# Attention inner loop: turns of four key tiles in place of pairs of two

## The reference

```python
DIM_HEAD, HEADS = 64, 16
q = (x @ Wq).reshape(b, s, HEADS, DIM_HEAD).transpose(0, 2, 1, 3)
k = (x @ Wk).reshape(b, s, HEADS, DIM_HEAD).transpose(0, 2, 1, 3)
v = (x @ Wv).reshape(b, s, HEADS, DIM_HEAD).transpose(0, 2, 1, 3)
scale = 1.0 / np.sqrt(np.sqrt(DIM_HEAD))
scores = jnp.einsum('bhqd,bhkd->bhqk', q * scale, k * scale)
weights = jax.nn.softmax(scores.astype(jnp.float32), axis=-1)
out = jnp.einsum('bhqk,bhkd->bhqd', weights, v)
return out.transpose(0, 2, 1, 3).reshape(b, s, HEADS * DIM_HEAD) @ Wo
```

## Time and profile before

| what | value |
|---|---|
| median of 3 runs | 3771.01 us (3770.84 to 3777.43) |
| time of the profiled execution | 3775.72 us |
| its span, first to last instruction | 3773.7 us |
| mean granted TensorE clock over the span | 0.954 |
| the two attention loops (first to last exponential) | 812.9 to about 2087 us, about 2187 to 3465.9 us |
| PE busy, 1200 to 1400 us | 199.43 of 200 us |
| DVE, ACT, POOL busy, 1200 to 1400 us | 124.77, 99.36, 174.44 us |
| copies of a finished group's output, first batch, 853.0 to 1464.6 us | 16, so 40.77 us a group |

### The profile page before, as it was taken

One profiled execution on the slowest core, in us unless ns is written; L12 is line 12 of the kernel. 1 busy time (PEld: TensorE's weight loads), 2 busy tenths in 40 slices (PEclk: granted clock), 3 DMA queues, 4 the chain that ended last, 5 costly groups with the idle time before them and its releaser, 6 DMA issues. The chain is left out here.

```text
span 3773.7 us, 48349 instructions
## 1 busy us (share of the span) xinstructions
PE 3348.8 (89%) x19009; PEld 1769.9 (47%) x19009; DVE 2411.6 (64%) x2756; ACT 1687.3 (45%) x2053; POOL 2768.3 (73%) x1154
## 2 busy tenths in 40 slices
PE   5674577379999999999999599999999999998798
PEld 2222222235554545455455245454554545454798
DVE  5998599766666665665664466666665665662554
ACT  4331433134454545445445345454545445544454
POOL 1783078238888888888889378888888888898233
PEclk9997799779999999999999799999999999999899
DMA  1330133010000000000000100000000000000000
GB/s 25 134 117 17 59 116 117 11 45 1 4 1 4 1 4 4 1 4 1 1 1 1 39 3 1 4 4 1 4 1 4 1 4 2 1 1 12 26 18 15
DMA packets 61536, 76.14 MB, mean 20 GB/s; under 512 B 7290, under 2 KB 48963, under 8 KB 61251
## 3 DMA queue, kind: packets, MB, share of 16 engines
q1 hardware_dynamic: 59362, 72.71, 6.0%
q10 hardware_dynamic: 1952, 0.43, 0.1%
HBM read 66.30 MB, written 6.82 MB: 19 GB/s over the span
## 5 line engine op out<-in xcount | busy, mean ns | idle before, releaser
L1311 POOL TENSOR_TENSOR den_g<-den_g,p 128x1024 f32<-128x1024 f32 x896 | 2129.0, 2376 | 292.4 <-ACT p L1287 184.8
L971 DVE TENSOR_REDUCE quarters<-psum 128x2 f32<-128x1024 f32 x1024 | 1250.3, 1224 | 941.8 <-PE psum L964 932.3
L1287 ACT ACTIVATE p<-psum 128x1024 f32<-128x1024 f32 x1024 | 994.8, 1023 | 725.8 <-PE psum L1190 719.5
L1201 PE MATMUL psum<-p,v 128*64 128x512 f32 x4096 | 991.4, 605 | 0.0
L964 PE MATMUL psum<-k_main,q_main 64*128 64x512 f32 x2048 | 462.5, 447 | 13.4 <-DVE quarters L971 10.9
L1201 PEld LDWEIGHTS psum<-p,v 128*64 128x64 f32 x4096 | 248.4, 136 | 469.7 <-issue 316.4
L1190 PE MATMUL psum<-q_main,k_main 64*128 64x512 f32 x2048 | 407.8, 394 | 4.5 <-PEq L1101 4.5
L1190 PE MATMUL psum<-q_rest,k_main 64*128 64x512 f32 x2048 | 404.7, 391 | 0.0
L1190 PE MATMUL psum<-q_main,k_rest 64*128 64x512 f32 x2048 | 404.5, 390 | 0.0
L1190 PE MATMUL psum<-row_shift,row_ones 64*128 64x512 f32 x2048 | 404.0, 389 | 0.0
L964 PEld LDWEIGHTS psum<-k_main,q_main 64*128 64x128 f32 x2048 | 193.6, 184 | 362.7 <-issue 198.6
(11 more groups left out here) (252 smaller groups left out, 3406.7 us busy)
## 6 DMA issues: line engine op xcount, KB each, us to landing
c_sb<-bc_rows SPq DMA_DIRECT2D x64, 512.0 KB, 3.5
work<-bc_rows SPq DMA_DIRECT2D x32, 512.0 KB, 4.9
resid<-in_resid SPq DMA_DIRECT2D x8, 256.0 KB, 3.3
x_mid<-resid SPq DMA_DIRECT2D x8, 256.0 KB, 2.6
xa<-x_mid SPq DMA_DIRECT2D x8, 256.0 KB, 3.5
x_tok<-x_mid SPq DMA_DIRECT2D x8, 256.0 KB, 3.7
x_mid<-x_tok SPq DMA_DIRECT2D x8, 256.0 KB, 2.7
x<-x_mid SPq DMA_DIRECT2D x8, 256.0 KB, 2.7
```

What stands on the lines that cost most here:

```text
L971: return nc.vector.reduce_max(quarters[:, :, n], max_banks.rearrange("p (h k) -> p h k", h=2), X_AXIS)
L1201: last = nc.tensor.matmul(o_bank[hi(h), :], vv[:, kt, hi(h)], p[:, u % LIVE, h, :], start=(kt == 0), stop=(kt == KT - 1))
L1287: nc.scalar.activation(flat(p[:, u % LIVE]), s_bank(u), ACT.Exp, scale=float(DH) ** -0.5).then_inc(p_ready, 1)
L1311: nc.gpsimd.tensor_tensor(sums, first, src, ALU.add).then_inc(added_g, 1)
```

## The change

TensorE's order is rewritten in turns of four units. In a turn, the 16 score steps of units first+2 to first+5 come in a row, with the four maxima of units first to first+3 before score steps 0, 5, 11 and behind step 15 (`MAX_AT`), then the values of the four units. A use of bank 7 stands either before the values of a turn or behind them. The jobs are renamed: each group has projections 0 and 1 (keys and queries, one each in turns 0 and 3, before the values) and "values" (turn 1, behind); `den` is behind turn 0, `out` before the values of turn 2, `shift` behind turn 2. Scores wait for the exponential at their first step and for the shift at their fourth. `LIVE` goes from 8 to 10. ScalarE and VectorE do their parts in the matching order: VectorE reads the four maxima of a turn, then does its parts of the bank's jobs and `make_shift`. The numbers of matmuls, exponentials, adds, readings and DMAs are the same.

```diff
-LIVE = 8
+LIVE = 10
...
-BANK7_AT = {0: 0, 2: "den", 8: "out", 10: "shift", 12: 1, 14: 2}
+TURN = 4
+TURNS = KT // TURN
+LEAD_S = 2
+
+BANK7_AT = {(0, "before"): 0, (0, "behind"): "den", (1, "behind"): "values", (2, "before"): "out",
+            (2, "behind"): "shift", (3, "before"): 1}
+
+MAX_AT = (0, 5, 11, 16)
...
-                def scores(u):
+                def score_steps(u):
...
-                    if kt == 0 and g:
-                        pe.wait_ge(shift_read, 2 * g)
-                    if u >= 2:
-                        pe.wait_ge(p_ready, u - 1)
...
                     for i, (left, right) in enumerate(terms):
+                        if i == 0 and u >= 2:
+                            pe.wait_ge(p_ready, u - 1)
+                        if i == 3 and kt == 0 and g:
+                            pe.wait_ge(shift_read, 2 * g)
                         for h in range(2):
                             last = nc.tensor.matmul(s_bank(u)[:, piece(h)], left[hi(h)], right[hi(h)],
                                                     start=(i == 0), stop=(i == len(terms) - 1))
-                    last.then_inc(s_psum, 1)
+                        if i == len(terms) - 1:
+                            last.then_inc(s_psum, 1)
+                        yield
...
-                scores(0)
-                scores(1)
-                for u in range(0, len(units), 2):
-                    maxes(u)
-                    if u + 2 < len(units):
-                        scores(u + 2)
-                        scores(u + 3)
-                    maxes(u + 1)
-                    values(u)
-                    values(u + 1)
-                    if u in at_unit:
-                        use_bank7(at_unit[u])
+                for u in range(LEAD_S):
+                    for _ in score_steps(u):
+                        pass
+                for i in turns:
+                    first = i * TURN
+                    ahead = range(first + LEAD_S, min(first + LEAD_S + TURN, len(units)))
+                    steps = (step for u in ahead for step in score_steps(u))
+                    for n in range(MAX_AT[-1] + 1):
+                        if n in MAX_AT:
+                            maxes(first + MAX_AT.index(n))
+                        next(steps, None)
+                    if (i, "before") in at_turn:
+                        use_bank7(at_turn[i, "before"])
+                    for u in range(first, first + TURN):
+                        values(u)
+                    if (i, "behind") in at_turn:
+                        use_bank7(at_turn[i, "behind"])
...
+                for i in turns:
+                    if (i - 1, "behind") in at_turn:
+                        read_bank7(at_turn[i - 1, "behind"])
+                    if i and i % TURNS == 0:
+                        copy_outputs(i // TURNS - 1)
+                    for u in range(i * TURN + LEAD_S, min((i + 1) * TURN + LEAD_S, len(units))):
+                        weigh(u)
+                    if (i, "before") in at_turn:
+                        read_bank7(at_turn[i, "before"])
...
+                for i in turns:
+                    g = i // TURNS
+                    for u in range(i * TURN, (i + 1) * TURN):
+                        if u in max_units:
+                            to, n = max_step(*units[u])
+                            dve.wait_ge(max_psum, u + 1)
+                            read_max(nc, quarters[:, to % 2], max_banks, n).then_inc(max_read, 1)
+                    k = at_turn.get((i, "before"))
+                    if k is not None and uses[k][0] == "out":
+                        add_outputs(k)
+                    elif k is not None:
+                        take_rest(k)
+                    if i % TURNS == SHIFT_MADE_AT // TURN and g + 1 < GC:
+                        dve.wait_ge(max_read, g * KT + SHIFT_MADE_AT)
                         if g:
                             dve.wait_ge(bank7_full, use_of["shift", g - 1] + 1)
                         make_shift(nc, st, quarters[:, (g + 1) % 2], maxima[:], shift).then_inc(shift_ready, 1)
...
+                    if (i - 1, "behind") in at_turn and uses[at_turn[i - 1, "behind"]][0] == "den":
+                        invert(g - 1)
+                        normalise(g - 1)
```

More of the change, by code:

```diff
@@ L1112, in attention_pairs @@
     units = [(g, kt) for g in range(GC) for kt in range(KT)]
+    turns = range(GC * TURNS)
     uses = []
[L1115 to L1126, removed]
+    for i in turns:
+        g = i // TURNS
+        for place in ("before", "behind"):
+            what = BANK7_AT.get((i % TURNS, place))
+            if what in ("den", "out"):
+                if g:
+                    uses.append((what, g - 1, i, place))
+            elif what == "shift":
+                if g + 1 < GC:
+                    uses.append((what, g, i, place))
+            elif what is not None and g + CHUNKS < GC:
+                uses.append((what, g, i, place))
+    at_turn = {(i, place): k for k, (what, g, i, place) in enumerate(uses)}
+    use_of = {(what, g): k for k, (what, g, i, place) in enumerate(uses)}
+    projection = lambda what, g: 2 * CHUNKS + g % CHUNKS if what == "values" else 2 * (g % CHUNKS) + what
     max_units = [u for u, (g, kt) in enumerate(units) if max_step(g, kt)[0] < GC]
@@ L1155, in _ @@
                     if pair:
-                        sp.wait_ge(bank7_full, use_of[2, CHUNKS * pair - 1] + 1)
+                        sp.wait_ge(bank7_full, use_of[1, CHUNKS * pair - 1] + 1)
                     for i, w in enumerate(("Wq", "Wk", "Wv")):
@@ L1205, in use_bank7 @@
                 def use_bank7(k):
-                    what, g, _ = uses[k]
+                    what, g, _, _ = uses[k]
                     if k:
@@ L1224, in use_bank7 @@
                             pe.wait_ge(weights, 48 * (g // CHUNKS))
-                        last = project(nc, bank7, w, xaT, 3 * (g % CHUNKS) + what)
+                        last = project(nc, bank7, w, xaT, projection(what, g))
                     last.then_inc(bank7_full, 1)
-                scores(0)
-                scores(1)
-                for u in range(0, len(units), 2):
-                    maxes(u)
-                    if u + 2 < len(units):
-                        scores(u + 2)
-                        scores(u + 3)
-                    maxes(u + 1)
-                    values(u)
-                    values(u + 1)
-                    if u in at_unit:
-                        use_bank7(at_unit[u])
+                for u in range(LEAD_S):
[15 more added lines that the diff above has]
+                        use_bank7(at_turn[i, "behind"])
             @block.scalar
@@ L1264, in read_bank7 @@
                     else:
-                        i = 3 * (g % CHUNKS) + what
+                        i = projection(what, g)
                         if i < 2 * CHUNKS:
@@ L1279, in copy_outputs, with weigh @@
                     nc.scalar.copy(o_raw[:], o_bank).then_inc(o_copied, 1)
-                for u, (g, kt) in enumerate(units):
+                def weigh(u):
                     act.wait_ge(s_psum, u + 1)
@@ L1350, in add_outputs @@
                         nc.vector.tensor_tensor(attnT[:, cols], attnT[:, cols], bank7, ALU.add).then_inc(bank7_free, 1)
-                for u, (g, kt) in enumerate(units):
-                    if kt == SHIFT_MADE_AT and g + 1 < GC:
-                        dve.wait_ge(max_read, u)
+                for i in turns:
+                    g = i // TURNS
+                    for u in range(i * TURN, (i + 1) * TURN):
[10 more added lines that the diff above has]
+                        dve.wait_ge(max_read, g * KT + SHIFT_MADE_AT)
                         if g:
```

## The result

The changed kernel takes 3926.86 us (median of 4 runs, 3924.5 to 3934.31) against 3772.59 for the kernel before, a ratio of 1.041 with a 95 % interval of 1.0392 to 1.0429: 4.1 % slower, 154 us. The forecast was 199 us and 3970 us, in a range of 3855 to 4035. The profiled executions differ by 158.6 us (3934.31 and 3775.72). All of it lies in the two attention loops, which take 163 us more; the rest of the program takes 5 us less. From its first to its last exponential a batch takes 1360.9 us (819.7 to 2180.6) and 1361.3 (2268.5 to 3629.8), against 1279.8 (812.9 to 2092.7) and 1279.0 (2186.9 to 3465.9) before.

What follows compares the result with a forecast made beforehand. TensorE was taken as the bound, busy 199.4 of 200 us in the attention loops. Terms: 203 (turns) + 4 (exponentials) - 20 + 12 (bank 7) = +199 us, forecast 3970 us, range 3855 to 4035.

Steps and rivals of the forecast that it cites:

- The mechanism: In a turn, each next maximum waits until VectorE has read the one bank pair: +203 us, longer turns' gain included.
- The handover's size: From one maximum's start to the next: 0.54 to the reading, 1.23 reading, 0.10 release, 1.87 us; low 1.71, high 1.92.
- halves: A maximum's two matmuls, taken to start one after the other behind values or a wait, 0.50 us for the pair.
- Bank 7: In the new places 56 projections and 40 sums of denominators no longer wait, 0.12 and 0.32 us each: -20 us.
- two new ones: Near waits at "values" behind turn 1 and the shift behind turn 2, 0.1 us each in 62 groups: +12 us.
- late shift: Rival: adding the outputs or `make_shift` ends 0.5 us later, each group waits: +31 us, 4001 us; chance 0.08.
- whole add: `make_shift`'s last instruction could wait for a whole GpSimd add, shift late by up to about 0.3 us a group, 19 us.
- The exponentials: At score step 8, hidden behind waiting maxima; in 11 turns without maxima 0.4 us short twice a turn: about +4 us.
- the trip: A turn of four saves one of two trips from scores to values and back: -0.37 us a turn.
- The exponential rival: The exponential, not the reading, holds TensorE up: turn 8.73 against 8.72 us, only bank 7's 20 us left, 3751; chance 0.05.
- The clock: Rival: TensorE's short pauses make the granted clock fall; low for a twentieth of the time, +100 us, 4071 us; chance 0.04.

Runs made afterwards that it cites:

- e8: The changed kernel with the maxima before score steps 0, 8 and 12 and behind step 15: 3990.69 us, ratio 1.0569 to the kernel before.
- e4: The changed kernel with maxima before steps 0 and 8, behind 15, and the fourth between the second and third unit's values: 3820.78 us, ratio 1.0125.
- e1: The changed kernel with VectorE reading only half of the columns of the maxima banks in the attention pairs: 3736.4 us, ratio 0.9906 to the kernel before.
- e9: The changed kernel with a quarter of the maxima columns read and maxima before score steps 0, 4, 8 and 12: 3684.06 us, ratio 0.9759.
- e2: The kernel before with VectorE reading only half of the maxima columns in the attention pairs, as a control: 3752.64 us, ratio 0.9946.

## Why the forecast held, and where its sizes were off

- **The mechanism** was right: the handover of the one pair of maxima banks sets the turn. The profile after shows it three times a turn; e8 moved the time up by 64 us where the gaps' rule gave 59; e4 and e1 took 106 and 190 us away by giving the handover room or making it short. That the turn is not slow for its length is shown by e4 and e9.
- **The handover's size.** Forecast 1.87 us, measured 1.82. The 0.54 to the reading's start and the 1.23 of reading were right; the release is 0.05 us as in the projection's row, where I took 0.10 between that and the 0.15 of the earlier trace rows. Three gaps are -0.15 us; the way from the fourth maximum to the values is 0.43 and not 0.35, +0.08; so the turn is 9.47 and not 9.55: 0.08 x 245 = 20 us of the 40 (199 - 158.6) that the forecast was too high beside the profiled run.
- **The "halves".** The forecast reads the 0.50 us of a maximum behind values or behind a wait as two matmuls that start one after the other. That reading is wrong, though the 0.34, 0.43 and 0.54 us that it goes with are measured and stand. A single matmul of L971 takes 497 ns in the median:

  ```profile
  L971 PE MATMUL psum<-k_main,q_main x2048: 393/497/793, 789.9 to 3585.2; 64*128 64x512 f32 x187
  ```

  So both matmuls of a pair whose row is 0.50 us long start together, within a few ns. What differs is the weight load: in the stream it starts 0.23 us ahead of its matmul (1330.40 and 1330.63 in the turn above), behind a wait together with it (1331.18 and 1331.19). In the first loop of the kernel before, the 504 long matmuls of maxima and scores (0.50 us) start within 0.003 us of their weight load, the 4488 short ones (0.39 us) 0.09 to 0.24 us behind it. That this load costs the 0.11 us is read from the rows; no run varies it.
- **Bank 7.** -20 for the waits that go, +12 for two new ones, together -8, was the forecast. The weight loads of the projections (L1004 now) and of the denominators (L1227) have no row with VectorE as releaser any more. The projection of values (L1006) has one, in 54 loads, but with the same 0.81 us idle that its loads show in e9, where VectorE is not named; VectorE's last step ends 3.83 us behind the fourth maximum, and TensorE comes at 4.02. Measured is 5.50 us a group in place of 5.90, about -25 us over 62 groups: no new wait came. "values" in turn 1 costs 10.58 - 9.47 = 1.11 us, and the shift finds its row ready in time, as this timeline of the changed kernel shows for one group:

```profile
1326.55 1.91 DVE L987 TENSOR_TENSOR shift<-maxima,shift 128x8 bf16<-128x8 f32 x1
...
1329.04 0.40 PE L995 MATMUL psum<-ident_bf,shift 128*2 128x128 bf16 x8
```

  The row is made at 1328.46 and needed at 1329.04. L987 takes 0.17 to 2.243 us, 1.934 in the median, so the long cases of the earlier trace rows are still there, but 0.6 us of room covers them here. No group shows a late shift: each of the 64 waits of L995's weight loads in the whole trace is put down to "issue" (nothing that the profile shows), none to VectorE.

  ```profile
  PEld psum L995 <- issue: 51.2, 64, 0.8
  ```

  Why L987 is long can be seen too. The add of GpSimd that was running when it started ends at 1326.08 + 2.35 = 1328.43, and L987 ends 0.03 us later:

  ```profile
  1326.08 2.35 POOL L1340 TENSOR_TENSOR den_g<-den_g,p 128x1024 f32<-128x1024 f32 x1
  ```

  So it is in 57 of its 64 cases; the other 7 take 0.17 us. It waits for what is left of a running add, which is less than the whole add that the forecast allowed for.
- **The exponentials.** In turns with maxima they were hidden, but for some hundredths (the weight load at 1333.50 us, 0.08 us ahead of a unit's first score step, shows 0.20 us idle with ScalarE named). Without maxima the forecast was two waits a turn, 0.8 us, less the trip. A clean turn there takes 7.98 us (2161.43 to 2169.41) against 7.84, +0.14. It has one wait, 0.62 us from step to step at score step 8; at step 12 the next exponential is no longer late. So +2 us in place of +4.
- **The sum with measured sizes**: 0.75 x 245 = 184 for the turns, -25 for bank 7, +2 for the turns without maxima, 161 us, against 163 us more between first and last exponentials of the two batches and 158.6 in the profiled runs. No large term is missing.
- **The rivals.** The exponential rival could not be seen in the changed kernel, but its price, 8.73 us a turn, was near to what e1 measured, 8.69. So the forecast's own sentence holds: had the reading been quick, the turns as placed would have gained next to nothing beyond bank 7 (e1 with 3736 us against e2 with 3753). The clock did not fall; the granted clock in the loop is 1.00 with three waits of 0.1 to 0.35 us in 9.5 us. The Trainium skill, "TensorE: Matmul & The Clock Gate", section "A second HAM failure mode: psum-queue depth-cycling", tells of a kernel in which frequent short idling made the clock swing. This trace shows no such swing in the loops.

## What to carry to other kernels

Before putting more work of one kind in a row, compute the handover of the buffer that this work goes through (write, read by the other engine, release) and compare it with the spacing that the new order offers. An average that fits (one reading of 1.23 us in 2.2 us a unit) says nothing once the work is bunched: with one buffer, n items in a row take at least n - 1 handovers, and the pause behind them (here the values) is no help. What stood to be saved here was 0.3 us a turn, and the waits cost 1.05 (9.47 less the 8.42 of e9); the same bank-7 gain was to be had in the old order by moving one VectorE step.

## What the runs showed that I had not expected

- A wait of TensorE costs more than its length here: behind it the weights are loaded as the matmul starts and not 0.23 us ahead, the pair takes 0.50 us in place of 0.39, and the next step comes after 0.34 in place of 0.23. A handover that started in the stream took 1.72 us and one that started from a wait 1.82 (e8), and the way from a waited maximum to the values 0.43 in place of 0.32 us.
- "Busy" hides such waits: in the changed kernel TensorE is busy 194.5 of 200 us, 97 %, though a turn of 9.47 us holds 1.05 that e9 does without.
- VectorE's last instruction for the shift works on 8 values a partition and takes 1.93 us in the median: in 57 of 64 cases it ends 0.03 us behind the end of an add of GpSimd. It had room here.
